# One product of 65 rows written as a product of 64 rows and one of a single row, 128 times in a two-stage feed-forward and attention kernel

## The chip, the cores and the metric

The program runs on one core of one Trainium2 chip. Its time is the device time of one execution in microseconds (us). A profile of one execution, with the start and length of every instruction, goes with it. Engines are named PE (TensorE, matrix products), PEld (its weight loads, which have their own rows), DVE (VectorE), ACT (ScalarE), POOL (GpSimd) and SP (the engine that issues most DMAs).

## The reference

The input x has 16 batches of 512 tokens with 256 features. Three blocks follow each other: a feed-forward block at half weight, an attention block with 16 heads of 16 features, and the same feed-forward block again. The feed-forward block has a dense base and, for each batch, one of eight adapters, chosen by the smallest reconstruction loss:

```
def _L0_ffn_ref(x, W_base, b_base, W_enc, b_enc, W_dec, b_dec, W_down, b_down, W_up, b_up, connected_idx):
    base = jnp.einsum('btd,de->bte', x, W_base) + b_base
    ...
    top1 = jnp.argmin(losses, axis=0)
    adp = connected_idx[top1]
    Wd, bd = (W_down[adp], b_down[adp])
    Wu, bu = (W_up[adp], b_up[adp])
    mid = jax.nn.relu(jnp.einsum('btd,bdr->btr', x, Wd) + bd[:, None, :])
    adapter_out = jnp.einsum('btr,brd->btd', mid, Wu) + bu[:, None, :]
    return base + adapter_out
...
x = x + 0.5 * _L0_ffn_ref(_layernorm(x, axis=-1), ...)
x = x + _L0_attn_ref(_layernorm(x, axis=-1), ...)
x = x + 0.5 * _L0_ffn_ref(_layernorm(x, axis=-1), ...)
```

`mid` has 64 units for each token. `mid @ Wu + bu` is the adapter's second product.

## The kernel before

The work of one batch is cut into stages with short names. Each engine walks its own written-out list of stages (`tensor_order`, `scalar_order`, `vector_order`, `gpsimd_order`, `sync_order`), with other lists for the first and the last batches, and engines meet through semaphores alone. One pass of the steady list advances one batch, and mixes stages of up to four batches. On PE the stages that matter here are these:

- `s1` (line 1680): scores for the row maxima, two bf16 products of 512 columns for a half. DVE reduces each (line 2076).
- `s2` (line 1692): the same scores with the maximum subtracted, two bf16 products for a half. ACT takes the exponential (line 1919).
- `pv` (line 1706): probabilities times values. Eight fp32 products, each of which fills 32 columns of PE's array; four of them, for four heads, stand side by side in the array.
- `en`, `gr`, `cost` (lines 1761, 1778 and 1780, 1789): the adapters' losses. `cost` is a product of 32 columns of the array over 8 moving columns.
- `dn` (line 1802): the chosen adapter's first product, on 64 columns of the array, in float32r (FR).
- `up` (lines 1821 and 1822): the base product and the chosen adapter's second one, which add up in one PSUM bank. This is the stage of the change.

`up(b, f, half)` handles half of a batch's 512 tokens for the first (f = 0) or second (f = 1) feed-forward block. For each of its two tiles of 128 tokens it runs six FR products of 256 moving columns (line 1821: two halves of the features, each as high by high, high by low and low by high part), then one plain fp32 product (line 1822). The latter has the tile of `mid` as its stationary operand and `wu` as the moving one. A plain fp32 product is two instructions in the profile, an FR or bf16 one a single instruction. `mid` and `wu` have R + 1 = 65 rows: 64 rows of units, and a row of ones in `mid` against a row with `b_up + b_base` in `wu`, so that the bias comes with the product. After the last product a semaphore releases DVE, which adds half of the bank to x (line 2175).

There are 16 batches, 2 blocks, 2 halves and 2 tiles: 128 products at line 1822. In the steady list of a batch, `up` stands four times, and what follows it on PE is `cost` once, `nt` (a fp32 transpose, line 1868) once, and `s2` (bf16) twice. Between the two tiles of a half the next row is again an FR product of line 1821.

The program's instructions carry a tile of the array: `s1`, `s2`, `en`, `gr` and line 1822 use the whole array, 128 rows by 128 columns; `pv` and `cost` use 128 rows by 32 columns; `dn` is written as 128 rows by 64 columns.

Of the kernel before, what the change touches and what calls it, by code (L numbers as in the profile page):

```python
# [31 lines left out]
N, R = 8, 64  # L32
# [39 lines left out]
def final(b):  # L72

    return b.number == B - 1


def initial(b):

    return b.number == 0


def slot(b, f):

    return 1 - f if b.number == (B - 1 if f else 1) else f
# [1322 lines left out]
def macaron(nc, x_in, Wq, bq, Wk, bk, Wv, bv, W0, b0, W_base, b_base, W_enc, b_enc, W_dec, b_dec, W_down, b_down,  # L1407
            W_up, b_up, connected_idx, const, out):
    with ExitStack() as ctx:
        def sb(name, shape, dt=F32):  # L1410
            return ctx.enter_context(nc.sbuf_tensor(name, shape, dt))
# [54 lines left out]
        wu = [t[0:R + 1, :] for t in wu_mT]  # L1466
        mT = wu_mT[0][96:128, 0:D // 2].bitcast(BF16).rearrange("p (k q) -> p k q", k=2)
        bdn = [sb(f"bdn{f}", [R, 1]) for f in range(2)]
        mid = [sb(f"mid{f}", [R + 1, S]) for f in range(2)]
# [38 lines left out]
        def up_bank(b, f, x):  # L1508

            return dense_bank(b, f, x if f else 1 + initial(b) * (1 - x))  # L1510
# [161 lines left out]
        def _(pe):  # L1672
# [133 lines left out]
            def up(b, f, half):  # L1806
                e = slot(b, f)
                bank = up_bank(b, f, half)
                if half == 0:
                    pe.wait_ge(*mid_done[f].at(b, 0))  # L1810
                    if f and b.number + 2 < B:
                        pe.wait_ge(*mT_done.at(b + 2, 0))
                elif slot(b, f) or not (initial(b) or final(b) and f):
                    pe.wait_ge(*up_done[f].at(b, 0))
                if initial(b) and f == 0:
                    pe.wait_ge(s_split, 2)
                for t in range(2 * half, 2 * half + 2):
                    o = bank[:, D * (t % 2):D * (t % 2) + D]
                    for c in range(C):
                        for n, (x, w) in enumerate(((xh, w_bh), (xh, w_bl), (xl, w_bh))):  # L1820
                            pe.matmul(o, x[e][:, c, 128 * t:128 * t + 128], w[:, c, :], start=(c == 0 and n == 0), stop=False)  # L1821
                    last = pe.matmul(o, mid[e][:, 128 * t:128 * t + 128], wu[e], start=False, stop=True)  # L1822
                last.then_inc(up_full[f].sem, 1)

            def project(b, k):
# [53 lines left out]
            def out_project(b, half):  # L1879
                bank = out_bank(b, half)  # L1880
                pe.wait_ge(*oT_done.at(b, C - 1))
                for t in range(2 * half, 2 * half + 2):
                    for c in range(C):
# [3 lines left out]

            do = dict(s1=s1, s2=s2, pv=pv, mt=maxima, tr=transposed, en=encode, gr=gram, cost=cost, dn=down,
                          up=up, qk=project, va=values, nt=natural, ot=out_transposed, op=out_project)

            pe.wait_ge(s_ident, 16)
            pe.wait_ge(s_decoder, 16 * DECODER_LOADS)
            for p in range(NP):
                for c in range(C):
                    last = pe.transpose(ps[:, c, 128 * p:128 * p + 128], w_dec[:, p, 128 * c:128 * c + 128], ident)
# [3 lines left out]
            for p in range(NP):  # L1899
# [3 lines left out]
                for c in range(C):  # L1903
                    w = raw[:, 2 + c, 128 * p:128 * p + 128]
                    last = pe.matmul(ps[:, 3, 8 * p:8 * p + N], w, bdec[:, c, :], start=(c == 0), stop=(c == C - 1))
# [458 lines left out]
```

## Time and profile before

| | |
|---|---|
| time, median of 3 runs | 1784.11 us (1783.69 to 1787.06) |
| the profiled execution's own time | 1784.44 us |
| its span, first to last instruction | 1782.6 us |
| PE busy | 1703.6 us, 96% of the span |
| DVE, ACT, POOL busy | 1265.2 us, 973.0 us, 497.0 us |
| mean granted TensorE clock | 0.988 of full speed |

The time has some 2 us around the span. A PE instruction is recorded with its whole way through the array, so neighbours overlap: what a product costs PE is read from the distance between starts, not from its length. When a bf16 or fp32 product is followed by an FR one, the FR row starts 25 ns after it and then takes its distance later; over such a pair only the sum of the two distances says something.

### The profile page before, as it was taken

To read this page: it belongs to the slowest core of one execution; us is meant where nothing else is said; L and a number is where in the kernel's file an instruction comes from. 1 tells how busy PE (TensorE), PEld (TensorE's weight loads), DVE (VectorE), ACT (ScalarE), POOL (GpSimd) and SP (SyncE) were. 2 spreads that over 40 slices of the span, in tenths; PEclk is the share of its full clock that TensorE was granted. 3 is DMA by queue.
4 is the path that set the end of the run, shared out by engine and by line. 5 is a ranking of instruction groups with operands and counts; after the bars stand their busy time and mean duration, and the time that the engine had idled before them with its cause. 6 is when DMAs were issued, how large, how long until landed. Compare 5 with 4: busy or idle time off the path is not lost.

```text
span 1782.6 us, 26353 instructions
## 1 busy us (share of the span) xinstructions
PE 1703.6 (96%) x9064; PEld 997.6 (56%) x9064; DVE 1265.2 (71%) x2829; ACT 973.0 (55%) x1954; POOL 497.0 (28%) x663
## 2 busy tenths in 40 slices
PE   5878999999999999999999999999999999999987
PEld 4624555556565565656556565655656565554345
DVE  6478786867768686776868677686867868576722
ACT  2326474655637465563746556474655647465551
POOL 2314060421406042140604215060421506023010
PEclk9889999999999999999999999999999999999999
DMA  5343342223334222343422234332233434224300
GB/s 133 48 71 72 37 82 32 62 40 60 72 49 79 35 61 42 61 72 48 76 36 62 43 61 72 48 75 36 61 45 60 72 48 75 32 33 70 44 1 24
DMA packets 96715, 99.37 MB, mean 56 GB/s; under 512 B 19972, under 2 KB 88261, under 8 KB 96453
## 3 DMA queue, kind: packets, MB, share of 16 engines
q1 hardware_dynamic: 93830, 97.16, 32.6%
q8 instruction: 72, 1.18, 0.3%
q10 hardware_dynamic: 2752, 0.54, 0.2%
q14 instruction: 61, 0.50, 0.1%
HBM read 63.54 MB, written 33.55 MB: 54 GB/s over the span
## 4 chain that ended last, share of the span: by engine, by line
PE 84%; DVE 8%; ACT 2%; issue 2%; POOL 2%; DMA 1%; SPq 0%; POOLq 0%; ACTq 0%; DVEq 0%
PE ps L1706 11%; PE ps L1692 11%; PE ps L1680 11%; PE ps L1778 10%; PE ps L1761 10%; PE ps L1780 6%; PE ps L1821 5%; PE ps L1837 5%; PE ps L1822 3%; PE ps L1802 3%; PE ps L1745 2%; PE ps L1847 2%; DVE mx L2076 2%; PE ps L1884 2%; PE ps L1868 2%
## 5 line engine op out<-in xcount | busy, mean ns | idle before, releaser
L2076 DVE TENSOR_REDUCE mx<-ps 128x1 f32<-128x512 f32 x1024 | 655.5, 683 | 258.8 <-PE ps L1680 257.6
L1919 ACT ACTIVATE pr<-ps 128x512 f32<-128x512 f32 x1024 | 557.3, 599 | 386.5 <-PE ps L1692 383.0
L1680 PE MATMUL ps<-stack 96*128 96x512 bf16 x1024 | 316.0, 384 | 12.4 <-DVE mx L2076 8.5
L1692 PE MATMUL ps<-stack 98*128 98x512 bf16 x1024 | 314.6, 384 | 9.2 <-ACT pr L1919 3.3
L1706 PE MATMUL ps<-pr,va 128*32 128x512 f32 x2048 | 247.7, 602 | 2.6 <-ACT pr L1919 2.3
L1692 PEld LDWEIGHTS ps<-stack 98*128 98x128 bf16 x1024 | 82.4, 98 | 184.5 <-issue 106.9
L1680 PEld LDWEIGHTS ps<-stack 96*128 96x128 bf16 x1024 | 95.2, 98 | 156.0 <-DVE mx L2076 50.9
L2321 POOL CAST wdh<-wd_all 128x128 fp32r x32 | 9.5, 297 | 585.2 <-DVE adapter L2165 557.4
L2131 DVE SCALAR_TENSOR_TENSOR ps<-ps,wb,h 128x512 f32<-128x512 f32 x128 | 96.5, 755 | 65.1 <-PE ps L1780 65.1
L1780 PE MATMUL ps<-h,gram_w 128*128 128x512 f32 x256 | 130.6, 592 | 0.0
L1706 PEld LDWEIGHTS ps<-pr,va 128*32 128x32 f32 x2048 | 53.7, 109 | 136.2 <-issue 131.2
L1778 PE MATMUL ps<-xh,w_dh 128*128 128x512 f32 x256 | 121.5, 475 | 6.8 <-DVE ps L2131 4.4
L1761 PE MATMUL ps<-xh,w_eh 128*128 128x512 f32 x256 | 123.6, 483 | 0.9 <-DVE xl L2118 0.9
L2248 POOL TENSOR_SCALAR rs<-mv 128x4 f32<-128x4 f32 x48 | 11.4, 237 | 404.7 <-DVE mv L2096 399.6
L1977 ACT ACTIVATE h<-ps,benc 128x512 f32<-128x512 f32 x128 | 87.1, 693 | 64.1 <-PE ps L1761 64.0
L2277 POOL TENSOR_TENSOR qb<-qb,cst 128x512 f32<-128x512 f32 x64 | 91.4, 1428 | 47.4 <-DVE qs L2191 46.9
L1761 PE MATMUL ps<-xl,w_eh 128*128 128x512 f32 x256 | 101.8, 398 | 0.0
L1761 PE MATMUL ps<-xh,w_el 128*128 128x512 f32 x256 | 101.6, 397 | 0.0
L1778 PE MATMUL ps<-xl,w_dh 128*128 128x512 f32 x256 | 101.2, 395 | 0.0
L1778 PE MATMUL ps<-xh,w_dl 128*128 128x512 f32 x256 | 101.1, 395 | 0.0
L2285 POOL TENSOR_TENSOR qb<-qb,parts 128x512 f32<-128x512 f32 x64 | 78.9, 1233 | 79.0 <-ACT parts L1998 79.0
L1821 PE MATMUL ps<-w_bh,xh 128*128 128x256 f32 x256 | 96.4, 376 | 1.5 <-ACT mid L1984 1.5
(153 smaller groups left out, 2951.5 us busy)
## 6 DMA issues: line engine op xcount, KB each, us to landing
stack<-scratch SPq DMA_DIRECT2D x384, 128.0 KB, 6.3
scratch<-parts SPq DMA_DIRECT2D x64, 384.0 KB, 2.6
xin<-in_L_attn_x_dram SPq DMA_DIRECT2D x15, 512.0 KB, 4.0
out_dram<-x SPq DMA_DIRECT2D x15, 512.0 KB, 8.8
stack<-wu_mT SPq DMA_DIRECT2D x128, 4.0 KB, 1.7
cst<-in_const_dram SPq DMA_DIRECT2D x1, 1024.0 KB
raw<-in_L_ffn_W_dec_dram ACTq DMA_DIRECT2D x1, 512.0 KB, 5.6
pr<-in_L_ffn_W_enc_dram SPq DMA_DIRECT2D x2, 256.0 KB, 7.6
```

Of the source, the lines that this page charges most:

```text
L1680: pe.matmul(bank1[:, t % 2, :], stack[0][0:KB, hd, 128 * t:128 * t + 128], stack[1][0:KB, hd, :], start=True, stop=True).then_inc(s1_full. ...
L1692: pe.matmul(bank2[:, a % 2, :], stack[1][:, 4 * g + a, 128 * t:128 * t + 128], stack[0][:, 4 * g + a, :], start=True, stop=True).then_inc( ...
L1706: last = pe.matmul(bank_o[32 * a:32 * a + 32, :], va[b.odd][:, t, 4 * g + a, :], held(b, n)[:, a, :], start=(t == 0), stop=(t == T - 1))
L1761: last = pe.matmul(bank, w[:, c, 2 * p:2 * p + 2, :].rearrange("p n r -> p (n r)"), x[e][:, c, :], start=(c == 0 and w is w_eh and x is xh ...
L1778: pe.matmul(bank, w[:, c, 128 * p:128 * p + 128], x[e][:, c, :], start=(c == 0 and w is w_dh and x is xh), stop=False)
L1780: pe.matmul(bank, gram_w[:, p, :], h[:, p, :], start=False, stop=True).then_inc(gr_full[f].sem, 1)
L1821: pe.matmul(o, x[e][:, c, 128 * t:128 * t + 128], w[:, c, :], start=(c == 0 and n == 0), stop=False)
L1837: last = pe.matmul(bank, y[:, c, 128 * m:128 * m + 128], x[:, c, :], start=(c == 0 and n == 0), stop=(c == C - 1 and n == 2))
L1919: act.activation(held(b, n)[:, a, :], bank2[:, a % 2, :], ACT.Exp, scale=SCALE).then_inc(ex_done.sem, 1)
L2076: dve.tensor_reduce(mx[:, hd // 4 % 2, e:e + 1], bank1[:, t % 2, :], AX.X, ALU.max).then_inc(mx_done.sem, 1)
L2131: dve.scalar_tensor_tensor(out=bank, in0=bank, scalar=wb2[:, p:p + 1], in1=h[:, p, :], op0=ALU.add, op1=ALU.mult, accum_out=r[e][:, p:p + ...
L2277: pool.tensor_tensor(q[:], q[:], v["cos"][:, S * (k // 2):S * (k // 2) + S], ALU.mult).then_inc(cos_done.sem, 1)
```

## The change

In `up`, the product of 65 rows becomes two that add to the same bank: one over the 64 rows of units and one over the single row of ones with the bias. The first no longer ends the accumulation, the second does, and the semaphore hangs on the second.

```
@@ -1819,7 +1819,8 @@
                     for c in range(C):
                         for n, (x, w) in enumerate(((xh, w_bh), (xh, w_bl), (xl, w_bh))):
                             pe.matmul(o, x[e][:, c, 128 * t:128 * t + 128], w[:, c, :], start=(c == 0 and n == 0), stop=False)
-                    last = pe.matmul(o, mid[e][:, 128 * t:128 * t + 128], wu[e], start=False, stop=True)
+                    pe.matmul(o, mid[e][0:R, 128 * t:128 * t + 128], wu[e][0:R], start=False, stop=False)
+                    last = pe.matmul(o, mid[e][R:R + 1, 128 * t:128 * t + 128], wu[e][R:R + 1], start=False, stop=True)
                 last.then_inc(up_full[f].sem, 1)
```

The built program gives the product of 64 rows a tile of 64 rows by 128 columns at row 0, and the single row a tile of 32 rows by 128 columns at row 64. Before, line 1822 had the tile of 128 by 128. No other product has a tile of fewer than 128 rows, before or after.

On PE, in the steady part of the program, one half of `up` with what stands before and behind it reads so before (`L1789` is `cost`, `L1692` and `L1680` are `s2` and `s1`; a plain fp32 product is one row here):

```order
L1692 MATMUL ps<-stack 128x512 x2
L1680 MATMUL ps<-stack 128x512 x2
L1821 MATMUL ps<-w_bh,xh 128x256
L1821 MATMUL ps<-w_bl,xh 128x256
L1821 MATMUL ps<-w_bh,xl 128x256
L1821 MATMUL ps<-w_bh,xh 128x256
L1821 MATMUL ps<-w_bl,xh 128x256
L1821 MATMUL ps<-w_bh,xl 128x256
L1822 MATMUL ps<-wu_mT,mid 128x256
L1821 MATMUL ps<-w_bh,xh 128x256
...
L1822 MATMUL ps<-wu_mT,mid 128x256
L1789 MATMUL ps<-z,va 32x8
L1692 MATMUL ps<-stack 128x512 x2
```

And now, from the first tile's end to the same `cost`:

```order
L1822 MATMUL ps<-wu_mT,mid 128x256
L1823 MATMUL ps<-wu_mT,mid 128x256
L1821 MATMUL ps<-w_bh,xh 128x256
...
L1822 MATMUL ps<-wu_mT,mid 128x256
L1823 MATMUL ps<-wu_mT,mid 128x256
L1789 MATMUL ps<-z,va 32x8
L1692 MATMUL ps<-stack 128x512 x2
```

Nothing has moved: a row of line 1823 stands behind each of the 128 rows of line 1822, and the other engines' lists are as they were. Below line 1822 every line number is one higher.

## Rows read from the trace of the kernel before

**Rows 1.** Page, busy time, share and instructions of each engine.

```profile
PE 1703.6 (96%) x9064; PEld 997.6 (56%) x9064; DVE 1265.2 (71%) x2829; ACT 973.0 (55%) x1954; POOL 497.0 (28%) x663
```

**Rows 2.** Stretches, the last a steady batch: length, busy us of PE, PEld, DVE, ACT, POOL, clock.

```profile
0.00:175.00 175.00, 129.94 (x583) 76.89 (x584) 116.50 (x263) 63.62 (x126) 58.96 (x68) 0.90 0.45 83
175.00:1550.00 1375.00, 1367.25 (x7420) 810.90 (x7418) 1022.98 (x2288) 795.72 (x1606) 398.83 (x533) 1.00 0.33 55
1550.00:1782.00 232.00, 206.36 (x1064) 109.78 (x1063) 125.74 (x280) 113.64 (x224) 39.18 (x62) 0.98 0.24 37
...
555.00:659.10 104.10, 103.60 (x565) 61.73 (x564) 77.80 (x175) 60.46 (x123) 30.64 (x41) 1.00 0.34 57
```

**Rows 3.** Waits of PE: engine line <- releaser: total us, times, longest us.

```profile
PE ps L1680 <- DVE mx L2076: 8.5, 26, 1.4
...
PE ps L1729 <- DVE x L2222: 6.2, 13, 0.7
```

**Rows 4.** Chain that ended last, one steady stretch: start us, us, what.

```profile
609.61 0.71 PE ps L1821 x6
610.32 0.43 PE ps L1822 x2
...
618.02 0.54 PE ps L1692 x2
...
627.99 0.45 PE ps L1822 x2
628.46 0.69 DVE x L2175
```

**Rows 5.** Timeline of DVE behind one `up`: start, us, row [idle before <-releaser].

```profile
611.93 0.69 DVE L2175 SCALAR_TENSOR_TENSOR x<-ps,x 128x512 f32<-128x512 f32 x1 [1.22 <-PE ps L1822]
```

**Rows 6.** PE's groups by shape: out<-in, partitions x elements, count | busy us, mean ns | idle.

```profile
L1822 PE MATMUL ps<-wu_mT,mid 65*128 65x256 f32 x256 | 77.3, 383 | 0.0
...
L1884 PE MATMUL ps<-w,oT 128*128 128x256 f32 x256 | 61.3, 382 | 0.0
```

**Rows 7.** Timeline of PE, from `s1` into `pv` and `cost` and out of them.

```profile
579.13 0.59 PE L1680 MATMUL ps<-stack 96*128 96x512 bf16 x2
579.65 1.92 PE L1706 MATMUL ps<-pr,va 128*32 128x512 f32 x16
581.39 0.20 PE L1789 MATMUL ps<-z,va 128*32 128x8 f32 x2
```

**Rows 8.** Timeline of PE, end of a half of `up` before `cost`.

```profile
611.30 0.60 PE L1822 MATMUL ps<-wu_mT,mid 65*128 65x256 f32 x2
611.83 0.23 PE L1789 MATMUL ps<-z,va 128*32 128x8 f32 x2
```

**Rows 9.** Timeline of PE, the one place where `up` follows `pv` directly.

```profile
1648.51 1.92 PE L1706 MATMUL ps<-pr,va 128*32 128x512 f32 x16
1650.37 0.38 PE L1821 MATMUL ps<-w_bh,xh 128*128 128x256 f32 x1
1650.59 0.28 PE L1821 MATMUL ps<-w_bl,xh 128*128 128x256 f32 x1
```

**Rows 10.** Timeline of the weight loads at that place, and inside `up` for comparison.

```profile
611.18 0.31 PEld L1822 LDWEIGHTS ps<-wu_mT,mid 65*128 65x128 f32 x2
...
1650.37 0.19 PEld L1821 LDWEIGHTS ps<-w_bh,xh 128*128 128x128 f32 x1 [0.84 <-issue]
```

**Rows 11.** Timeline of PE, from `s1` into `dn`, on 64 columns.

```profile
599.37 0.60 PE L1680 MATMUL ps<-stack 96*128 96x512 bf16 x2
...
600.03 0.39 PE L1802 MATMUL ps<-xh,wdl 128*64 128x512 f32 x1
```

**Rows 12.** Timeline of PE, first batch, an `up` partly at the lower clock.

```profile
45.64 1.06 PE L1822 MATMUL ps<-wu_mT,mid 65*128 65x256 f32 x2
...
46.71 0.41 PE L1821 MATMUL ps<-w_bl,xh 128*128 128x256 f32 x1
```

More of the change, by code:

```diff
@@ L1821, in up @@
                             pe.matmul(o, x[e][:, c, 128 * t:128 * t + 128], w[:, c, :], start=(c == 0 and n == 0), stop=False)
-                    last = pe.matmul(o, mid[e][:, 128 * t:128 * t + 128], wu[e], start=False, stop=True)
+                    pe.matmul(o, mid[e][0:R, 128 * t:128 * t + 128], wu[e][0:R], start=False, stop=False)
+                    last = pe.matmul(o, mid[e][R:R + 1, 128 * t:128 * t + 128], wu[e][R:R + 1], start=False, stop=True)
                 last.then_inc(up_full[f].sem, 1)
```

## The prediction, made before the changed kernel ran

> **What bounds the kernel now.** I read the busy shares first. PE is busy for 96% of the span, DVE for 71%, ACT for 55% [rows 1]. A mean over stages can mislead, so I took windows: one steady batch lasts 104.10 us, PE is busy for 103.6 of them, and DVE for 77.8 [rows 2]. From 175 to 1,550 us, which is 13 such batches, PE is busy for 1367 of 1375 us [rows 2]. Then the waits of PE: its longest regular ones are 8.5 us on the row maxima, in 26 places, and 6.2 us in 13 places before `mt` (line 1729) [rows 3]. That is half a microsecond for each batch. In the steady part the chain that ended last runs from PE row to PE row [rows 4]. So PE's queue sets the pace, and a microsecond added to it is a microsecond added to the time unless it falls where PE would have waited anyway.
>
> The reader should see a second thing in the chain: it gives costs by distance, which recorded lengths (0.38 us for one instruction) do not. Six FR products of 256 columns take 0.71 us, 0.12 each; the fp32 product of line 1822, two instructions, takes 0.43; two bf16 products of 512 columns take 0.43 as well [rows 4].
>
> **What the change adds, step by step.** It removes nothing from PE. The product of 64 rows streams the same 256 columns as the one of 65 did. Rows do not enter the price: an fp32 instruction of 256 columns takes 383 ns with 65 rows and 382 ns with 128 [rows 6]. So the old product costs what it cost, 0.43 us, and the single row costs 0.43 us more, full price for one row. That is the first term: 128 x 0.43 = 55 us.
>
> The second term is the tile. Line 1822 had the whole array, as its neighbours have. Now it has 64 rows at row 0, then 32 rows at row 64, then the next instruction has the whole array again: three changes of the tile's shape for each tile of tokens. The trace has no product on fewer than 128 rows, but it has changes of the number of columns, in `pv` and `cost`:
>
> - Into 32 columns from `s1`: two bf16 products start at 579.13, and `pv` at 579.65 [rows 7]. That is 0.52 us where 0.43 would do, so 0.09 lost. Into `cost` from line 1822: 611.30 to 611.83, 0.53 in place of 0.43, 0.10 lost [rows 8].
> - Out of 32 columns into an FR product: `pv` to line 1821 takes 1650.37 - 1648.51 = 1.86 us [rows 9], where `pv` to `cost`, of the same shape, takes 1.74 [rows 7]; 0.12 lost, some 0.02 of it because four products stand side by side and end one after another. Behind it the first FR product has 0.22 us to the next start, not 0.12 [rows 9]: another 0.10. The weight load shows why. Inside `up` a load starts 0.12 us ahead of its product (611.18 against 611.30) [rows 8, 10]; here it starts with its product, at 1650.37, after PEld has stood idle for 0.84 us [rows 9, 10]. Across the change of shape the load isn't issued ahead, so its streaming lies bare.
> - Out of 32 columns into bf16: behind `pv`, two products of `s2` take 0.54 us in the chain, not 0.43 [rows 4]: 0.11 for both together.
>
> So I read a change of shape as 0.10 us of emptying the array plus the load of the next weights, 0.10 for 128 columns of fp32 or FR, about 0.01 for bf16. The weights of both new products have 128 columns of fp32.
>
> The Trainium skill, TensorEngine Tiling (Array Packing), section Key Properties, says the same of the first half in general: "Changing tiling mode (not just tile) drains the TensorE", and lists 64 x 128 and 32 x 128 as modes of their own. The trace agrees for 128 x 32, with 0.09 and 0.10 us [rows 7, 8]; for row tiles no run here shows it yet.
>
> One row speaks against the reading. `dn` is written on 64 columns, and from `s1` into it nothing is lost: two bf16 products at 599.37 and the first FR one together take until 600.03, 0.66 us [rows 11], which is 0.43 and one FR product of 512 columns at 0.23, twice the 0.12 of 256 columns. Either a tile of 64 columns is no new shape for an FR product, or some changes of shape are free. For the plain fp32 products of the change I go by `pv` and `cost`, which are plain fp32 too.
>
> The sum for a steady batch, by what comes behind each of its 8 products: four are followed by the next tile's FR product, 0.43 + 3 x 0.20 = 1.03 us each; two by `s2` in bf16, 0.43 + 0.40 + 0.11 = 0.94; one by fp32 transposes, taken between these prices, 0.98; one by `cost`, which pays for its own change of shape already, 0.43 + 0.40 = 0.83. Together 4.12 + 1.88 + 0.98 + 0.83 = 7.8 us, and 16 batches give 125 us.
>
> **What hides some of it.** In the steady part nothing: the one wait of PE, before `mt` of line 1729, is on DVE, and the chain to it starts with the last `up` at 627.99, goes on with DVE's addition at 628.46 [rows 4] and so starts later by as much as PE does. DVE is no cover either: behind `up` it had been idle for 1.22 us when PE released it [rows 5]. Before 175 us PE is busy for 130 us of 175, and after 1,550 us for 206 of 232 [rows 2], so it has gaps there, and 26 of the 128 products lie in these stretches. I take 3 us off for these, and add 1 us for the first batch, where two instructions take 1.07 us to the second next start (45.64 to 46.71) at half the clock [rows 12], so that four products cost nearly twice the price. In all 123 us. The profiled execution took 1784.4 us, 0.3 above the median, so the sum stands as well against the median: 1784.1 + 123 = 1907 us. Its own uncertainty is 0.08 us for each product: 10 us both ways.
>
> Bounds of the unknown, the price of a change of shape among row tiles: nothing, as `dn` has it, or 0.20 us, as line 1821 behind `pv` has it; 0.10 if the load can still be issued ahead. I take 0.20 because line 1821 behind `pv` is the nearest row: a change between plain fp32 and FR, with 128 columns of weights behind it [rows 9]. Below nothing it can go only if the two products overlap, which is the third rival.
>
> **Rivals.**
>
> 1. Cheaper changes (1865 to 1897). The array empties but the load of the next weights isn't bared, 3 x 0.10: 128 x 0.73 = 93 us, 1877. Or one of the three changes is free, 0.43 + 0.40: 106 us, 1890. For it: the load of the second product goes to other rows of the array than the first one uses. Against it: the bared load where line 1821 follows `pv` [rows 9, 10].
>
> 2. Changes of row tiles are free, as `dn` [rows 11]: 55 us, 1839 us. Against it: the holes before `pv` and `cost` [rows 7, 8].
>
> 3. Side by side. The four products of `pv`, on different columns, fill 1.74 us with 16 instructions [rows 7], which is four times 0.43: each group of four costs as much as one. If the product of 64 rows and that of the single row, on different rows of the array, stood side by side in that way, the added one would cost nothing, and with free changes the kernel would stay at 1784 us, the other side. It decides if the second product starts within a few ns of the first. Against it: both have different shapes, and both add to the same words of PSUM, while the products of `pv` go to different partitions.
>
> The Trainium skill, PSUM — Partial Sum Buffer, in PSUM bank collisions raise a hardware error, says that TensorE's writes from different row tiles of one tiling mode into one bank raise an error. Of tiles of two modes it says nothing there, and no run here shows either.
>
> 4. The clock. It is at 1.00 from 175 to 1,550 us [rows 2], the upper one of 2.4 GHz. A batch's 8 tiles of `up` will last 8 x (0.71 + 1.03) = 14 us, with holes. If these brought it to 1.2 GHz for half of that time, 7 us at half speed, 3.5 us would be lost in each batch and 56 in all: 1963 us. Against it: `pv` has holes too, and the clock stays.
>
> **Chances.** The forecast has 0.56, rival 1 0.23, rival 2 0.11, rival 3 0.03, rival 4 0.03, and 0.04 for what I haven't seen. The likeliest one's own range is 1897 to 1917. The range reaches down to rival 2, since the price of the changes is not in the trace, and up to 1922: 1836 to 1922. About 0.2%, 3.6 us, is what a measurement of this kernel can tell from no change. Every case but the third rival is slower by far more: slower 0.97, same 0.02, faster 0.01.
>
> **What would show it.** In the changed profile line 1823 should have 256 instructions of 1 row with a mean near 380 to 480 ns; the distance from a tile's first instruction of line 1822 to the next FR product's second start should grow from 0.43 + 0.12 = 0.55 us to about 0.55 + 1.03 = 1.58. The first load of each of the lines 1822 and 1823, and of the product behind, should start with its product and no longer 0.12 us ahead. A steady batch should last 104.1 + 7.8 = 111.9 us, with DVE, ACT and POOL as busy in it as before, and a clock of 1.00. The forecast is wrong if line 1823 starts within some ns of line 1822 (rival 3), if the batch lasts 107.5 us (rival 2) or 110 us (rival 1), or if waits on DVE or DMA grow.

## The result, and the profile after

The changed kernel takes 1941.61 us (median of 4 runs, 1935.37 to 1944.64) against 1784.01: a ratio of 1.0875, 95% interval 1.0845 to 1.0904. It is 158 us slower. The forecast was 1907 us in a range of 1836 to 1922, so the direction was right and the growth of 123 us too small by 35, which puts the time outside the range. The profiled execution took 1935.37 us with a span of 1933.6; before it was 1784.44 and 1782.6.

The page of the changed kernel, busy time of each engine, and the clock in 40 slices:

```profile
PE 1859.2 (96%) x9320; PEld 1045.7 (54%) x9320; DVE 1266.6 (66%) x2829; ACT 973.9 (50%) x1954; POOL 495.9 (26%) x663
...
PEclk9879999999999999999999999999999999999997
```

PE has 256 instructions more and 156 us more of busy time than before [rows 1]. DVE, ACT and POOL do what they did. PE doesn't wait more: its idle time is 74.4 us of the span, and was 79.0. Its longest regular waits are about as before [rows 3], first one row of the kernel before that rows 3 don't show, then the rows of the changed kernel:

```profile
PE ps L1789 <- DVE z L2140: 4.0, 3, 1.4
```

```profile
PE ps L1680 <- DVE mx L2077: 7.2, 27, 0.9
PE ps L1789 <- DVE z L2141: 5.3, 4, 1.4
PE ps L1729 <- DVE x L2223: 4.7, 12, 0.7
```

Now the place of the change. The chain of the changed kernel in a steady batch (start us, us, what) answers to rows 4:

```profile
653.31 0.71 PE ps L1821 x6
654.02 0.63 PE ps L1822 x2
654.64 0.62 PE ps L1823 x2
655.27 0.90 PE ps L1821 x6
656.17 0.62 PE ps L1822 x2
```

The 64 rows take 0.63 us where 65 rows took 0.43, the single row takes 0.62, and the six base products behind it 0.90, not 0.71. The sum of the three differences is 0.20 + 0.62 + 0.19 = 1.01 us for each tile of tokens; the prediction had 1.03. The timeline of PE, and that of its weight loads, show how the time goes:

```profile
653.74 0.28 PE L1821 MATMUL ps<-w_bh,xl 128*128 128x256 f32 x1
653.95 0.70 PE L1822 MATMUL ps<-wu_mT,mid 64*128 64x256 f32 x2
654.57 0.69 PE L1823 MATMUL ps<-wu_mT,mid 1*128 1x256 f32 x2
655.20 0.39 PE L1821 MATMUL ps<-w_bh,xh 128*128 128x256 f32 x1
655.42 0.28 PE L1821 MATMUL ps<-w_bl,xh 128*128 128x256 f32 x1
```

```profile
653.62 0.19 PEld L1821 LDWEIGHTS ps<-w_bh,xl 128*128 128x128 f32 x1
653.95 0.29 PEld L1822 LDWEIGHTS ps<-wu_mT,mid 64*128 64x128 f32 x2
654.57 0.29 PEld L1823 LDWEIGHTS ps<-wu_mT,mid 1*128 1x128 f32 x2 [0.33 <-issue]
655.20 0.19 PEld L1821 LDWEIGHTS ps<-w_bh,xh 128*128 128x128 f32 x1 [0.33 <-issue]
```

The last base product starts at 653.74 and needs 0.12 us; the 64 rows start at 653.95, 0.09 late. At all three changes of shape the load starts with its product (653.95, 654.57, 655.20), where inside the base products it starts 0.12 us ahead (653.62 for 653.74). That is what rows 9 and 10 had shown for a change out of 32 columns.

One batch without any fall of the clock (a change from 2.4 to 1.2 GHz) lasts 111.65 us from its first `s1` to the next batch's, against 104.08 before, read in the same way: 7.57 us more; the prediction had 7.8. Two stretches of the changed kernel, each about as long as a batch (columns as in rows 2, and behind the clock the DMA's share and GB/s):

```profile
673.40:785.10 111.70, 111.63 (x573) 63.92 (x573) 76.85 (x172) 59.49 (x120) 30.63 (x41) 0.98 0.25 46
1122.10:1233.70 111.60, 110.64 (x578) 63.41 (x577) 77.29 (x174) 60.34 (x122) 30.64 (x41) 1.00 0.31 52
```

In the second the clock is at 1.00, in the first at 0.98: it holds one low stretch. A batch with one such stretch takes 113.3 us from start to start, 1.65 us more. Before, the clock was at 1.00 in all of the steady part [rows 2]. 16 x 7.57 = 121 us of the 151 in the profiled spans are products and changes of shape. The other 30 go with the clock, and they sit in three places:

- In the 11 batches in the middle, 97.5 us were added, of which 83 are 11 x 7.57. The granted clock has 8 low stretches there, 31 us in all, and none before. A low microsecond does half the work, so 31 of them cost about 15: it fits the 14 that are left.
- At the start (the first two batches), 17.7 us were added, 15.1 of them products; the low time grew by 17 us, but only 2.6 us are left for it: part of it falls on waits.
- At the end (the last three batches), 35.7 us were added, 22.7 of them products, and the low time grew by 23 us, which at half speed would cost 11.5 of the 13 that are left. The last 25.4 us of the program run at half the clock throughout, the last `up` with them.

The end of the changed kernel:

```profile
1908.20:1933.60 25.40, 18.38 (x46) 10.56 (x46) 1.38 (x2) 0.68 (x1) 1.21 (x4) 0.50 0.06 21
```

The timeline shows what a fall looks like in the middle. This one comes in the second single row of a half, and everything behind it has twice its distance:

```profile
661.66 0.38 PE L1822 MATMUL ps<-wu_mT,mid 64*128 64x256 f32 x1
661.96 0.89 PE L1823 MATMUL ps<-wu_mT,mid 1*128 1x256 f32 x2
662.78 1.03 PE L1692 MATMUL ps<-stack 98*128 98x512 bf16 x2
663.61 1.06 PE L1680 MATMUL ps<-stack 96*128 96x512 bf16 x2
```

From `s2` to `s1` there are 0.83 us; at the full clock it is 0.43. All eight falls in the middle come at this place: 0.4 to 1.2 us after the start of a half's second single row, so four of them in it and four just behind it, in `s2` or `s1`.

### The profile page after: what moved, and what is told of

It is laid out like the page before. It is cut to its first block, busy times and chain, and to the rows that moved or that the text cites. A ratio compares the mean times of both kernels' runs of the same rounds, so it can differ in the third digit from the quotient of the medians.

```text
span 1933.6 us, 26865 instructions
## 1 busy us (share of the span) xinstructions
PE 1859.2 (96%) x9320; PEld 1045.7 (54%) x9320; DVE 1266.6 (66%) x2829; ACT 973.9 (50%) x1954; POOL 495.9 (26%) x663
## 4 chain that ended last, share of the span: by engine, by line
PE 86%; DVE 7%; ACT 2%; issue 2%; POOL 2%; DMA 1%; POOLq 0%; SPq 0%; ACTq 0%; DVEq 0%
PE ps L1706 11%; PE ps L1692 10%; PE ps L1680 10%; PE ps L1778 10%; PE ps L1761 9%; PE ps L1821 6%; PE ps L1780 6%; PE ps L1823 4%; PE ps L1822 4%; PE ps L1838 4%; PE ps L1802 3%; PE ps L1745 2%; PE ps L1848 2%; DVE mx L2077 2%; PE ps L1885 2%
## 5 line engine op out<-in xcount | busy, mean ns | idle before, releaser
L1680 PE MATMUL ps<-stack 96*128 96x512 bf16 x1024 | 321.0, 389 | 10.4 <-DVE mx L2077 7.2
L1692 PE MATMUL ps<-stack 98*128 98x512 bf16 x1024 | 317.7, 387 | 9.0 <-ACT pr L1920 3.8
L1706 PE MATMUL ps<-pr,va 128*32 128x512 f32 x2048 | 255.9, 619 | 2.7 <-ACT pr L1920 2.6
L1692 PEld LDWEIGHTS ps<-stack 98*128 98x128 bf16 x1024 | 80.5, 98 | 192.1 <-issue 118.7
L1680 PEld LDWEIGHTS ps<-stack 96*128 96x128 bf16 x1024 | 95.9, 99 | 156.4 <-DVE mx L2077 49.6
L1821 PE MATMUL ps<-w_bh,xh 128*128 128x256 f32 x256 | 92.4, 361 | 1.5 <-ACT mid L1985 1.5
```

Source lines behind the costliest of these rows:

```text
L1680: pe.matmul(bank1[:, t % 2, :], stack[0][0:KB, hd, 128 * t:128 * t + 128], stack[1][0:KB, hd, :], start=True, stop=True).then_inc(s1_full. ...
L1692: pe.matmul(bank2[:, a % 2, :], stack[1][:, 4 * g + a, 128 * t:128 * t + 128], stack[0][:, 4 * g + a, :], start=True, stop=True).then_inc( ...
L1706: last = pe.matmul(bank_o[32 * a:32 * a + 32, :], va[b.odd][:, t, 4 * g + a, :], held(b, n)[:, a, :], start=(t == 0), stop=(t == T - 1))
```

## The experiments

Twelve kernels ran. A table first; "batch" is a steady batch from start to start, the shortest of those in the middle; "low" is the time at 1.2 GHz within the 11 batches in the middle. In e3, e4, e6, e9, e10 and e12 each batch has low time, the shortest too, so there "batch" is more than products and changes of shape alone. The ratio is against runs of the kernel before on the same chip (medians 1784.0 to 1785.7 us), not against the first row. The expectations count low stretches over two batches more, one at either side: 9 and 41, where the middle has 8 (the changed kernel) and 36 (e6).

| kernel | added per tile of tokens | us | ratio (95%) | batch us | low us |
|---|---|---|---|---|---|
| before | | 1784.0 | | 104.08 | 0 |
| changed | 1 product, 3 changes | 1941.6 | 1.0875 (1.0845 to 1.0904) | 111.65 | 31 |
| e1 | 1 product, 0 changes | 1844.9 | 1.0332 (1.0305 to 1.0359) | 107.53 | 0 |
| e2 | 0 products, 2 changes | 1837.6 | 1.0280 (1.0252 to 1.0309) | 106.64 | 0 |
| e5 | 0 products, 2 changes | 1835.5 | 1.0282 (1.0264 to 1.0301) | 106.62 | 0 |
| e3 | 1 product, 5 changes | 2073.3 | 1.1588 (1.1530 to 1.1645) | 119.57 | 150 |
| e4 | 1 product, 2 changes | 1930.6 | 1.0814 (1.0785 to 1.0844) | 112.20 | 48 |
| e8 | 2 tiny products, 4 changes | 1889.7 | 1.0576 (1.0552 to 1.0600) | 109.77 | 0 |
| e7 | 3 products, 3 changes | 2055.4 | 1.1514 (1.1494 to 1.1535) | 119.11 | 0 |
| e6 | 3 products, 3 changes | 2247.3 | 1.2615 (1.2575 to 1.2655) | 129.45 | 348 |
| e10 | 3 products, 3 changes | 2263.9 | 1.2669 (1.2610 to 1.2727) | 129.42 | 382 |
| e9 | 3 products, 3 changes | 2172.6 | 1.2154 (1.2106 to 1.2203) | 121.79 | 219 |
| e11 | 3 products, 2 changes | 2012.1 | 1.1281 (1.1216 to 1.1345) | 117.01 | 0 |
| e12 | as changed, in half of the tiles | 1871.2 | 1.0480 (1.0431 to 1.0528) | 109.17 | 38 |

### The price of a product and of a change of shape

**e1: the product of 65 rows twice.**

```
+                    pe.matmul(o, mid[e][:, 128 * t:128 * t + 128], wu[e], start=False, stop=False)
                     last = pe.matmul(o, mid[e][:, 128 * t:128 * t + 128], wu[e], start=False, stop=True)
```

> Line 1822 twice, each time with all 65 rows and the whole array: a second fp32 product without any change of the tile's shape (the adapter's part is counted twice). Theory 'tile' (an added product costs 0.43 us, each change of shape 0.20 more, and the falls of the clock come with the changed tiles): 128 x 0.43 = 55 us, 1839 us, clock 0.988 as before, a steady batch of 104.1 + 3.4 = 107.5 us. Rival 'more work' (any added small fp32 product costs about 1.0 us with what it disturbs): near 1910 to 1940 us.

Measured: 1844.9 us where 1839 was expected, and 107.53 us for a batch, 3.45 more than before, which is 8 x 0.43. The middle stretch:

```profile
278.10:1462.00 1183.90, 1177.73 (x6383) 711.67 (x6383) 856.12 (x1914) 664.79 (x1342) 337.03 (x451) 1.00 0.32 55
```

The added product alone is 16 x 3.45 = 55 us of the 158; in the middle the clock stays at 1.00. At both ends the low time grew from 43 to 60 us, with no change of shape and no product of few rows.

**e2: the 64 rows alone.**

```
-                    last = pe.matmul(o, mid[e][:, 128 * t:128 * t + 128], wu[e], start=False, stop=True)
+                    last = pe.matmul(o, mid[e][0:R, 128 * t:128 * t + 128], wu[e][0:R], start=False, stop=True)
```

> The product of 64 rows alone; the row of ones with the bias is left out. One product as before, but two changes of shape for each tile of tokens. Theory 'tile': no added product, per batch 4 x 0.40 + 2 x 0.31 + 0.30 + 0.20 = 2.7 us, 16 batches 44 us, 1828 us without any fall of the clock. If holes or tiles of few rows bring the clock down, some us more and a clock under 0.985. Rival 'the single row is what costs': 1784 us.

Measured: 1837.6 us. The batch took 2.56 us more (2.7 expected), 41 us in 16 batches; no fall in the middle. The rest of the 52 us against the runs before on that chip lies at both ends, where the low time grew from 43 to 74 us. That one product of the same columns costs 2.56 us more in each batch for having one row less shows the price of the changes of shape by itself. Its timeline:

```profile
643.48 0.28 PE L1821 MATMUL ps<-w_bh,xl 128*128 128x256 f32 x1
643.69 0.70 PE L1822 MATMUL ps<-wu_mT,mid 64*128 64x256 f32 x2
644.32 0.38 PE L1821 MATMUL ps<-w_bh,xh 128*128 128x256 f32 x1
644.54 0.28 PE L1821 MATMUL ps<-w_bl,xh 128*128 128x256 f32 x1
```

From 643.48 to 643.69 is 0.21 for a product of 0.12, then 0.63 for one of 0.43, then 0.22 for one of 0.12: 0.39 in all for two changes.

**e5: the single row alone.**

```
+                    last = pe.matmul(o, mid[e][R:R + 1, 128 * t:128 * t + 128], wu[e][R:R + 1], start=False, stop=True)
```

> The single row alone; the product of 64 rows is left out. Two changes of shape for each tile of tokens, as with the 64 rows alone (1837.6 us, clock 0.98). Theory 'tile': rows don't enter the price, 1837 us and 106.65 us for a steady batch. If a product of few rows brings the clock down by itself, the steady batches here show stretches at the lower clock that those of the 64 rows alone did not.

Measured: 1835.5 us, 106.62 us for a batch: one row costs what 64 rows do, and nothing falls in the middle. A single product of one row in a tile of tokens doesn't bring the clock down there.

**e3: both new products cut by columns.**

```
+                    for k, q in enumerate((slice(0, D // 2), slice(D // 2, D))):
+                        pe.matmul(o[:, q], mid[e][0:R, 128 * t:128 * t + 128], wu[e][0:R, q], start=False, stop=False)
+                        last = pe.matmul(o[:, q], mid[e][R:R + 1, 128 * t:128 * t + 128], wu[e][R:R + 1, q], start=False, stop=k == 1)
```

> Both new products cut in two by columns: 64 rows on columns 0 to 127, the single row on them, then both again for columns 128 to 255. The same number of streamed columns, but five changes of shape in place of three. Theory 'tile': 2 x 0.20 x 128 = 51 us over the changed kernel, 1992 us, and more if the clock falls oftener; by a drain without a bared load (0.10 each) 1967 us; by rival 'columns alone set the price' 1941 us.

Measured: 2073.3 us, 80 more than the changes of shape alone would make it. The timeline has these at their price, 0.41 us from product to product of 128 columns, 0.21 of it streaming:

```profile
693.04 0.48 PE L1823 MATMUL ps<-wu_mT,mid 64*128 64x128 f32 x2
693.46 0.48 PE L1824 MATMUL ps<-wu_mT,mid 1*128 1x128 f32 x2
693.87 0.48 PE L1823 MATMUL ps<-wu_mT,mid 64*128 64x128 f32 x2
694.29 0.48 PE L1824 MATMUL ps<-wu_mT,mid 1*128 1x128 f32 x2
...
696.43 0.79 PE L1823 MATMUL ps<-wu_mT,mid 64*128 64x128 f32 x2
697.15 0.79 PE L1824 MATMUL ps<-wu_mT,mid 1*128 1x128 f32 x2
```

The last two rows are at the lower clock, 0.72 apart. The rest is the clock: it is low for 150 us of the 11 batches in the middle. So here the expectation's first number was a lower bound, and the clock, which the prediction had at 3 in 100, weighs more here than in the changed kernel.

**e4: both single rows of a half side by side.**

```
+                    units = (mid[e][0:R, 128 * t:128 * t + 128], wu[e][0:R])
+                    one = (mid[e][R:R + 1, 128 * t:128 * t + 128], wu[e][R:R + 1])
...
+                    parts_ = [one, units, *base] if t % 2 else [*base, units, one]
```

> The changed kernel with the second tile of each half turned round: the single row first, then the 64 rows, then the six base products, so that both single rows stand side by side. The same products, four changes of shape in a half in place of six. Theory 'tile': a half loses 0.86 + 4 x 0.20 = 1.66 us against before in place of 1.95, 64 halves save 18 us: 1923 us, less if the clock falls less often. Rival 'more work': 1941 us.

Measured: 1930.6 us, 11 less than the changed kernel and not 18. The four products in a row:

```profile
650.75 0.28 PE L1825 MATMUL ps<-w_bh,xl 128*128 128x256 f32 x1
650.96 2.38 PE L1825 MATMUL ps<-wu_mT,mid 64*128 64x256 f32 x8
653.27 0.38 PE L1825 MATMUL ps<-w_bh,xh 128*128 128x256 f32 x1
```

2.31 us from 650.96 to 653.27 are 4 x 0.43 + 3 x 0.20, within 0.01: between the two single rows, which have the same tile, nothing is lost. But every steady batch in the middle has a fall, 48 us in all against 31. So fewer changes with all the thin work together give back part of what they save.

### What brings the clock down

Two theories were left: the holes at the changes of shape (the 0.2 us in which nothing streams), or the products of few rows.

**e6: the single row three times.**

```
+                    pe.matmul(o, mid[e][0:R, 128 * t:128 * t + 128], wu[e][0:R], start=False, stop=False)
+                    pe.matmul(o, mid[e][R:R + 1, 128 * t:128 * t + 128], wu[e][R:R + 1], start=False, stop=False)
+                    pe.matmul(o, mid[e][R:R + 1, 128 * t:128 * t + 128], wu[e][R:R + 1], start=False, stop=False)
+                    last = pe.matmul(o, mid[e][R:R + 1, 128 * t:128 * t + 128], wu[e][R:R + 1], start=False, stop=True)
```

> The changed kernel with the single row's product three times (the bias counts three times). No more changes of shape than in the changed kernel, but 2 x 0.43 us more for each tile of tokens: 110 us over it, 2051 us at an unchanged clock. Theory 'thin rows' (products of few rows count for little where the clock is decided): many more low stretches than the changed kernel's 9 in the steady part, clock under 0.95, 2080 us or more. Theory 'holes' (the emptied array at each change does it): the holes are spread over more time, so no more low stretches, 2051 us or less.

**e7: two products of 65 rows in place of the two added single rows.**

```
-                    pe.matmul(o, mid[e][R:R + 1, 128 * t:128 * t + 128], wu[e][R:R + 1], start=False, stop=False)
-                    last = pe.matmul(o, mid[e][R:R + 1, 128 * t:128 * t + 128], wu[e][R:R + 1], start=False, stop=True)
+                    pe.matmul(o, mid[e][:, 128 * t:128 * t + 128], wu[e], start=False, stop=False)
+                    last = pe.matmul(o, mid[e][:, 128 * t:128 * t + 128], wu[e], start=False, stop=True)
```

> The changed kernel with two products of all 65 rows on the whole array behind the single row (the adapter's part counts three times). The same three changes of shape and the same columns streamed as with the single row three times, but none of the added products is thin: 2051 us at an unchanged clock by both theories; fewer low stretches than the single row three times if thin rows decide, as many if holes do.

Measured: 2247.3 against 2055.4 us. Both stream the same columns over the same number of changes of shape; 192 us lie between them. Their middle stretches, e6 first:

```profile
312.90:1776.60 1463.70, 1462.72 (x6735) 851.63 (x6735) 860.06 (x1914) 665.82 (x1342) 337.03 (x451) 0.88 0.26 44
```

```profile
311.70:1622.80 1311.10, 1304.90 (x6734) 769.11 (x6733) 856.23 (x1914) 664.77 (x1342) 337.02 (x451) 1.00 0.30 50
```

PE is busy all the time in e6, and yet the clock is at 0.88. In e7, the two whole-array products leave it at 1.00 in the middle, higher than in the changed kernel itself, which has the same thin products and changes of shape without them. A busy PE row is therefore not what holds the clock. What differs between the two is one row on a tile of 32 rows against 65 rows on the whole array, with as many holes. At the ends e7 does no better: over the whole program its clock is 0.970, as in the changed kernel.

**e8: changes of shape without thin products.**

```
                         for n, (x, w) in enumerate(((xh, w_bh), (xh, w_bl), (xl, w_bh))):
                             pe.matmul(o, x[e][:, c, 128 * t:128 * t + 128], w[:, c, :], start=(c == 0 and n == 0), stop=False)
+                        pe.matmul(o[0:32, 0:N], ones, v["half"], start=False, stop=False)
```

> The kernel before with, behind each three base products, a product of 8 columns on a tile of 128 rows by 32 columns (it adds something to 8 columns of 32 tokens). Four changes of shape for each tile of tokens and no product of few rows. Per tiny product 0.09 + 0.05 + 0.09 and 0.10 for the bared load, some 0.33 us, 256 of them: 85 us, 1870 us. Theory 'holes': the clock falls in the steady part at least as often as in the changed kernel (9 stretches), 1890 us or more. Theory 'thin rows': no low stretch in the steady part, clock 0.985 or more.

Measured: 1889.7 us. A tiny product and the two changes around it:

```profile
643.50 0.28 PE L1821 MATMUL ps<-w_bh,xl 128*128 128x256 f32 x1
643.71 0.23 PE L1822 MATMUL ps<-cst,va 128*32 128x8 f32 x2
643.87 0.39 PE L1821 MATMUL ps<-w_bh,xh 128*128 128x256 f32 x1
644.09 0.28 PE L1821 MATMUL ps<-w_bl,xh 128*128 128x256 f32 x1
```

The time is the one that "holes" had given, but not for its reason. 109.77 us a batch are 5.69 more, 0.36 for each tiny product and not 0.33, which makes 91 us in 16 batches, and in the middle no stretch is low, as "thin rows" had it:

```profile
287.80:1496.10 1208.30, 1202.14 (x6559) 713.95 (x6559) 856.00 (x1914) 665.25 (x1342) 337.39 (x451) 1.00 0.32 54
0.00:287.80 287.80, 245.38 (x1143) 141.62 (x1144) 191.31 (x431) 120.52 (x240) 88.51 (x105) 0.89 0.38 69
```

Its mean clock is 0.975, not the 0.985 of "thin rows": in the first batches, where PE waits anyway, the low time grew from 34 to 65 us. Whether the holes do that isn't shown: there e1 has 44 us without any, the changed kernel 51 with three in each tile, and e5 68 with two, each in one profiled execution. But in the steady part four holes in each tile without a thin product bring nothing down.

**e9 to e11: how many rows.** The 64 rows, then three products more of 32, 1 or 64 rows, all at row 0 of the array (k in the lines below; the bias is left out in all three).

```
+                    pe.matmul(o, mid[e][0:R, 128 * t:128 * t + 128], wu[e][0:R], start=False, stop=False)
+                    pe.matmul(o, mid[e][0:k, 128 * t:128 * t + 128], wu[e][0:k], start=False, stop=False)
...
+                    last = pe.matmul(o, mid[e][0:k, 128 * t:128 * t + 128], wu[e][0:k], start=False, stop=True)
```

> The product of 64 rows and then three of the first 32 rows of units, in place of the single row three times (2247.3 us, clock 0.877, 41 low stretches in the steady part). The bias is left out. The tile of the array is of the same shape, 32 rows by 128 columns, at row 0, all 32 of its rows in use. Theory 'rows in use' (it is the few rows at work that bring the clock down): clearly fewer low stretches than 41, 2060 to 2150 us. Theory 'tile shape' (any tile of 32 rows does): as before, near 2247 us and 0.877.

> The product of 64 rows and then three of the first row of units alone. The bias is left out. As the single row of ones three times, but at row 0 of the array and with changing data in place of ones. If neither place nor data matter: 2247 us, clock 0.877. If the constant ones were the cause: near 2055 us, as with two whole-array products more.

> The product of 64 rows four times, bias left out. Two changes of shape, 3 x 0.43 us more for each tile of tokens than the 64 rows alone: 1837.6 + 165 = 2003 us and a steady batch of 106.65 + 10.3 = 117.0 us if the clock stays. Theory 'rows in use': few low stretches or none in the steady part. Theory 'tile shape': many, 2100 us or more.

Measured, for 1, 32 and 64 rows: 2263.9, 2172.6 and 2012.1 us, and 382, 219 and 0 us of low time in the middle. The middle stretch of e9, then that of e11:

```profile
308.30:1713.60 1405.30, 1401.88 (x6734) 822.55 (x6734) 858.18 (x1914) 665.13 (x1342) 337.01 (x451) 0.92 0.27 46
```

```profile
299.20:1587.40 1288.20, 1283.09 (x6735) 776.41 (x6735) 856.29 (x1914) 664.74 (x1342) 336.96 (x451) 1.00 0.30 50
```

One row at row 0 with changing data (e10) does about as one row of ones at row 64 (e6, 2247.3 us and 348 us low), so place and data don't decide. 32 rows in the same shape of tile do clearly less harm than one row (25 low stretches in the middle, against 33 in e10 and 36 in e6), so it isn't the shape alone, but more than expected (2150 us was the upper end), so either the rows in use don't act in simple proportion or the shape has a part in it. 64 rows bring nothing down, with one change of shape fewer than the others and a tile of 64 rows; which of the three does it, these runs don't separate. The batch of 117.01 us is the expected one; of the 9 us over the expected 2003, nothing lies in the middle.

**e12: the change in the first block alone.**

```
+                    if f:
+                        last = pe.matmul(o, mid[e][:, 128 * t:128 * t + 128], wu[e], start=False, stop=True)
+                    else:
...
```

> The change in the first feed-forward block alone, 64 of the 128 products. The steady batch has 4 of the 8: half of 7.56 us, 107.9 us. If the clock fell for each product by itself, half of what it takes in the changed kernel is left: 1784.5 + 157 / 2 = 1863 us. If it takes several halves close together, fewer low stretches than half: 1845 to 1855 us.

Measured: 1871.2 us, above both numbers, and 109.17 us for the shortest batch, which has a fall in it, against 107.9. The expectation that half of the change has half of the falls or fewer was wrong: there are 11 in the 11 batches in the middle, 38 us, against 31 with the whole change. Each steady batch has one fall, in the same place, 0.5 to 1.2 us after the start of a second single row of the first block. So how often the clock falls does not grow steadily with the thin work, and these runs don't settle what else counts.

## Why the prediction was wrong

**What bounds it: right.** PE's queue did set the pace. PE is busy for 96% of the span as before, its idle time did not grow, and the batch grew by what PE got.

**The added product, 128 x 0.43 = 55 us: right.** e1 has 3.45 us a batch, 55 us in 16. Rows don't enter: e2 and e5, with 64 rows and one, are 0.02 us a batch apart.

**The changes of shape, 0.20 us each: right.** This was the disputed price, taken from `pv` and line 1821 [rows 7, 9] with the load bared [rows 10]. The chain has 1.01 us for each tile where the sum had 1.03; the batch 7.57 where it had 7.8, 121 us where it had 125. The free change into `dn` [rows 11] was rightly not followed: for the plain fp32 products of few rows each change is paid. Rivals 1 and 2, cheaper or free changes, are out by the loads that start with their products, and rival 3 by starts 0.62 us apart.

**What hides some of it: 2 us off, not borne out.** The first and last batches gave 53 us for five batches, of which 38 are products and changes of shape at their full price. So on balance nothing was hidden. How much of the products the waits there did take in can't be told, as the clock fell for longer in the same batches.

**The clock: this is the step that failed.** The sum put it at nothing. The prediction had it as rival 4, in the right place (`up`, a fall in a batch) but by holes alone, with 3 in 100 and "`pv` has holes too, and the clock stays". That argument compares holes. But `pv` works on all 128 rows, and the runs show that in the steady part the products of few rows decide: with as many holes, products of one row brought the clock to 0.88 where whole-array ones left it at 1.00 (e6, e7), and four holes in each tile without a thin product left it at 1.00 (e8). Whether thin products would do it without any hole, no run shows; each has a change of shape at either side. In the changed kernel's profiled execution the clock goes with 30 us. Some 14 of them are the eight falls in the middle, which this explains. The other 16 lie at both ends, where the low time grew also without products of few rows (e1, e8); what decides there stays open. The median of the four executions is 6 us above the profiled one, and the others had a mean clock of 0.965 to 0.966 where it had 0.970. Rival 4's size, 56 us, was too large. The sum with the clock's 30 us would have been 1937.

**The range.** It reached down to a case that was unlikely and up by 15 us only. Its upper end was little more than the sum's own error of 10 us; the one case above it had been priced and was then left out as improbable. With a term that no row of before bears on (a product of few rows had never run), the range had to take it in.

## What to carry to other kernels

In these runs a product costs its columns, not its rows, and a change of the tile's shape costs an emptied array and the bared load of the next weights besides, 0.2 us here for 128 columns of fp32. So a bias belongs as one more row in a product that is there anyway, even if 65 rows need the whole array where 64 rows would not: splitting it off added 1.01 us to a product of 0.43. Between neighbours that use the whole array, even the 64 rows alone were dearer than the 65 (e2). And where PE streams through few rows for a good part of a stage, look at the granted clock: busy shares near 100% don't say that it holds.

## What had not been expected of the hardware

- TensorE's clock falls with PE busy by its rows all the time: PE 1462.7 of 1463.7 us busy and a clock of 0.88 (e6), as against 1.00 with the same columns on the whole array (e7). The holes at changes of shape don't show in the busy time, since the rows overlap; both kernels have as many.
- The effect is graded: three products of 1, 32 or 64 rows for each tile gave 382, 219 and 0 us of low time in the same 11 batches (the last with one change of shape fewer).
- Half of the thin work gave more falls than all of it (11 in e12, 8 in the changed kernel), and so did gathering it (14 in e4). In the changed kernel and in e12 they come at the end of a half of `up`; why in some batches and not in others is open.
- A tile of 128 rows by 64 columns in FR is entered without loss [rows 11], while tiles of 64 rows and of 32 rows in plain fp32 are not. Whether the number type or the shape makes the difference was not tried.
